# The middle stage of a gated two-layer model on one core: when the row means, the norms' roots and the small inputs are worked on

## The reference

```python
x = x + tanh(g_xattn[0]) * L0_xattn(ctx, ctx, layernorm(x), ssm_kernel, D, 8)   # long convolution per head
x = x + tanh(g_ffn[0])   * L0_ffn(layernorm(x), sim_matrix, gates, w_q, w_k, w_v, o_weights)
x = x + tanh(g_xattn[1]) * L1_xattn(layernorm(x), ctx, ctx)                     # attention, 8 heads
x = x + tanh(g_ffn[1])   * L1_ffn(layernorm(x), w_router, w_fc, w_proj)         # 8 experts, top 2

def L0_ffn(h, sim, gates, w_v, o_weights):          # 32 experts of width 64
    rep = mean(h, axis=1)                           # one row of 512 for each of the 16 sequences
    affinity = (rep / norm(rep)) @ (sim / norm(sim, axis=0))
    gated = relu(affinity - sigmoid(gates)); mask = gated > 0   # with a fallback to the top 16
    routing = softmax(where(mask, gated, -max))     # (16, 32)
    combined = einsum('be,bteh->bth', routing, einsum('btc,ehc->bteh', h, w_v) * mask)
    w_o_dyn  = einsum('be,ehd->bhd', routing, o_weights)
    return einsum('bth,bhd->btd', combined, w_o_dyn)
```

## Time and profile before

| | us |
|---|---|
| median of 3 runs | 1640.89 |
| lowest, highest | 1640.22, 1643.83 |
| profiled execution | 1636.78 |
| its span | 1635.1 |
| granted clock, mean of the span | 0.978 |
| PE busy | 1529.5 (94%) |
| VectorE, ScalarE, POOL busy | 1193.2, 978.7, 1032.5 |

### The profile page before, as it was taken

How to read it: one execution, slowest core, us unless ns; L and a number is a source line. 1 busy time by engine, 2 the same in 40 slices (tenths; PEclk the granted TensorE clock), 3 DMA queues, 4 the chain that set the end, 5 groups by cost and what they waited for, 6 DMA issues and landing times.

```text
span 1635.1 us, 28566 instructions
## 1 busy us (share of the span) xinstructions
PE 1529.5 (94%) x8923; PEld 1073.6 (66%) x8923; DVE 1193.2 (73%) x1863; ACT 978.7 (60%) x1527; POOL 1032.5 (63%) x855
## 2 busy tenths in 40 slices
PE   4999999997698899999999999889999999999996
PEld 4677777775464644444444444368999999999995
DVE  7788888888637667777777777266777777777774
ACT  6433333334624278888888887646777777776773
POOL 4788888885305478888888887601555555555553
PEclk9999999998899999999999999989999999999998
DMA  7333444436634876777777773391444444444443
GB/s 254 113 136 133 134 135 138 141 131 159 178 76 177 194 169 181 185 202 188 184 204 186 189 194 92 115 341 61 70 79 79 77 79 75 76 79 77 78 79 52
DMA packets 110843, 224.27 MB, mean 137 GB/s; under 512 B 12704, under 2 KB 12704, under 8 KB 109856
## 3 DMA queue, kind: packets, MB, share of 16 engines
q1 hardware_dynamic: 94848, 185.88, 40.0%
q0 software_dynamic: 15904, 37.23, 12.8%
HBM read 146.71 MB, written 75.84 MB: 136 GB/s over the span
## 4 chain that ended last, share of the span: by engine, by line
PE 34%; DMA 23%; issue 4%; DVE 3%; ACT 2%; POOL 1%; ACTq 0%; POOLq 0%; SPq 0%; DVEq 0%
DMA out_rows<-XN,slots 21%; PE pB L1433 10%; PE pO L1443 8%; PE pA L1415 7%; PE pO L1456 4%; DMA XN<-normed_rows,slots 1%; PE pO L1606 1%; PE pA L1594 1%; PE pB L1424 1%; POOL out_rows L1399 1%; PE pA L1511 1%; DVE low L1787 1%; PE pO L112 1%; PE pA L1518 0%; DVE XN L1976 0%
## 5 line engine op out<-in xcount | busy, mean ns | idle before, releaser
L1787 DVE TENSOR_REDUCE low<-pA 128x2 f32<-128x1024 f32 x256 | 306.9, 1223 | 112.2 <-PE pA L1415 98.4
L1680 ACT ACTIVATE pt<-pB 128x512 f32<-128x512 f32 x512 | 287.3, 593 | 88.6 <-PE pB L1433 80.4
L436 PE MATMUL y<-kv,toep 128*128 128x288 f32 x1280 | 326.1, 411 | 9.0 <-DVEq L63 5.8
L1399 POOL DMA_INDIRECT out_rows<-XN,slots x71 | 195.6, 2755 | 211.4 <-DMA out_rows<-XN,slots 172.5
L436 PEld LDWEIGHTS y<-kv,toep 128*128 128x128 f32 x1280 | 238.0, 190 | 96.9 <-DVEq L63 34.1
L1594 PEld LDWEIGHTS pA<-XN,fc 128*128 128x128 f32 x2272 | 264.3, 192 | 8.0 <-issue 2.7
L1594 PE MATMUL pA<-XN,fc 128*128 128x128 f32 x2272 | 265.1, 275 | 2.1 <-DVE XN L1956 1.1
L1433 PE MATMUL pB<-qs,ks 98*128 98x512 f32 x512 | 226.9, 446 | 3.7 <-ACT pt L1680 2.4
L1433 PEld LDWEIGHTS pB<-qs,ks 98*128 98x128 f32 x512 | 95.3, 188 | 193.9 <-ACT pt L1680 153.0
L406 ACT ACTIVATE ym<-y 128x384 f32<-128x384 f32 (+1 forms) x128 | 52.5, 410 | 229.0 <-PE y L436 229.0
L1746 ACT ACTIVATE proj_high<-WP 128x2048 fp32r x71 | 135.7, 1912 | 81.4 <-PE pO L1606 81.4
(11 more groups left out here) (285 smaller groups left out, 2509.8 us busy)
## 6 DMA issues: line engine op xcount, KB each, us to landing
ks<-ctx_high SPq DMA_DIRECT2D x64, 256.0 KB, 4.5
qs<-q_high SPq DMA_DIRECT2D x64, 256.0 KB, 6.1
kc<-in_ctx_conv SPq DMA_DIRECT2D x32, 384.0 KB, 5.5
XN<-in_x SPq DMA_DIRECT2D x16, 512.0 KB, 10.4
toep<-kernel_and_skip SPq DMA_DIRECT2D x32, 256.0 KB, 3.5
ct<-in_ctx SPq DMA_DIRECT2D x16, 512.0 KB, 6.3
ctx_high<-kh SPq DMA_DIRECT2D x16, 512.0 KB, 4.4
ctx_low<-kl SPq DMA_DIRECT2D x16, 512.0 KB, 5.1
```

What stands on the lines that cost most here:

```text
L436: m = pe.matmul(y[half].rearrange("p (l n) c -> p l n c", l=CB)[:, l, :, 0:PAIRS], toep[u][:, (l - s) * P:(l - s + 1) * P], kv[u][:, half, ...
L1399: pool.indirect_dma_start(out=out["out"], out_offset=bass.IndirectOffsetOnAxis(ap=slots[:, j:j + 1], axis=0), in_=ys[j % 2], in_offset=Non ...
L1680: act.activation(pt[s][:, h, :], bank(u, n), ACT.Exp, scale=SCALE1).then_inc(s_exp, 1)
L1787: dve.tensor_reduce(ap(low[u % 2], t % CB * NH + t // CB, [[NH, 2], [1, 1]]), pA[n % 2], op=ALU.max, axis=AX.X, negate=True).then_inc(s_re ...
```

## The change

- At the end of the convolution stage PE makes 23 products of the identity with 112 columns of itself into unused columns of y[0], behind s_tt = 2*H0 + 3.
- The groups of roots are now six: (8, 20) is split into (8, 16) and (16, 20). POOL finishes a group behind take(hi + 6) instead of take(hi + 4), the group of rows 24 to 27 behind the loop.
- The last group's roots are finished by VectorE (`last_roots`, with one operation less) right behind its loop; ScalarE makes their guess ahead of keep(31), and its last six weights instead of its last four follow the loop.
- The means' products are issued by fours (`means(i)`): behind forth(15), (17), (23), (25), (27) and (31), the last two fours behind the loop; each waits for its group's spread alone (six of the seven counts).
- The squares of sim and the sigmoid (`early`) stand behind iteration 4 of VectorE's loop, the products for the norms of sim behind forth(7).
- SP waits for five fours instead of two groups before it loads w_o: the same rows, 0 to 19.

```diff
--- before.py
+++ after.py
@@ -440,6 +440,11 @@
                                 if l in (1, 2):
                                     m.then_inc(s_yp, 1)
                             m.then_inc(s_y, 1)
+                unused = 64 - PAIRS
+                pe.wait_ge(s_tt, 2 * H0 + 3)
+                for _ in range(23):
+                    pe.matmul(ap(y[0], PAIRS, [[64, 4], [1, unused]]), ident,
+                              ident[:, 0:4 * unused].rearrange("p (n c) -> p n c", c=unused), start=True, stop=True)
 
             @block.vector
             def _(dve):
@@ -499,8 +504,9 @@
         with ExitStack() as st:
 
             GR = HR // 4
-            GROUPS3 = [(0, 8), (8, 20), (20, 24), (24, 28), (28, 32)]
+            GROUPS3 = [(0, 8), (8, 16), (16, 20), (20, 24), (24, 28), (28, 32)]
             LAST = len(GROUPS3) - 1
+            QUAD_AT = {15: 0, 17: 1, 23: 2, 25: 3, 27: 4, 31: 5}
             PAIRSB = B // 2
             HELD = range(TH, TH + B // 2)
             ORDER = [0] + list(range(1 + PAIRSB // 2, PAIRSB)) + list(range(1, 1 + PAIRSB // 2))
@@ -599,7 +605,7 @@
                     sp.wait_ge(s_x1, TH * b + TH)
                     sp.dma_start(X1[n].rearrange("(th p) c -> p th c", p=P), rows_of(b)).then_inc(s_hold, 16)
                 sp.wait_ge(s_hold, 16 * len(HELD))
-                sp.wait_ge(s_srm, 2)
+                sp.wait_ge(s_srm, (TH * HELD[-1] + TH) // 4)
                 for hq in range(HQ):
                     sp.dma_start(WOin[hq * E0:(hq + 1) * E0], a["w_o"][:, hq * HR:(hq + 1) * HR, :]).then_inc(s_wo, 16)
                 for n in range(HR // GR):
@@ -684,7 +690,7 @@
                 for j in range(3, UNITS):
                     take(j)
                     for g, (lo, hi) in enumerate(GROUPS3):
-                        if j == hi + 4:
+                        if j == hi + 6:
                             first(g)
                     if j == 5:
                         pool.wait_ge(s_ot, j + 1)
@@ -692,7 +698,6 @@
                                            pattern=[[1, E0], [-1, E0]], channel_multiplier=0).then_inc(s_con, 1)
                         pool.wait_ge(s_con, CONS)
                 first(LAST - 1)
-                first(LAST)
                 def add_row(n):
                     j = ROUND[2 * n + 1]
                     pool.wait_ge(s_part, n + 1)
@@ -724,13 +729,21 @@
                         m = pe.transpose(ph[j % 3][:, k * P:(k + 1) * P], ap(XN, j * ROW + k * P, [[1, P]]), ident)
                     m.then_inc(s_t2, 1)
 
-                def means(q):
-                    pe.wait_ge(s_rs, STEPS * (q + 1))
-                    for i in range(GROUPS3[q][0] // 4, GROUPS3[q][1] // 4):
-                        for g in range(4):
-                            m = pe.matmul(pS[g * E0:(g + 1) * E0, :], spread[:, 4 * i + g, :], row(4 * i + g),
-                                          start=(i == 0), stop=(i == UNITS // 4 - 1))
+                def means(i):
+
+                    q = [lo <= 4 * i < hi for lo, hi in GROUPS3].index(True)
+                    pe.wait_ge(s_rs, STEPS * q + STEPS - 1)
+                    for g in range(4):
+                        m = pe.matmul(pS[g * E0:(g + 1) * E0, :], spread[:, 4 * i + g, :], row(4 * i + g),
+                                      start=(i == 0), stop=(i == UNITS // 4 - 1))
                     m.then_inc(s_srm, 1)
+
+                def affinity_norms():
+                    pe.wait_ge(s_e0, 1)
+                    pe.wait_ge(s_con, 5)
+                    for k in range(CB):
+                        m = pe.matmul(p_e, ones, sim2[:, k, :], start=(k == 0), stop=(k == CB - 1))
+                    m.then_inc(s_pe, 1)
 
                 def inner(s):
                     p = ORDER[s]
@@ -756,20 +769,16 @@
 
                 back(0)
                 back(1)
-                pe.wait_ge(s_e0, 1)
-                pe.wait_ge(s_con, 5)
-                for k in range(CB):
-                    m = pe.matmul(p_e, ones, sim2[:, k, :], start=(k == 0), stop=(k == CB - 1))
-                m.then_inc(s_pe, 1)
                 for j in range(UNITS):
                     if j + 2 < UNITS:
                         back(j + 2)
                     forth(j)
-                    for g, (lo, hi) in enumerate(GROUPS3):
-                        if j == hi + 4:
-                            means(g)
-                means(LAST - 1)
-                means(LAST)
+                    if j == 7:
+                        affinity_norms()
+                    if j in QUAD_AT:
+                        means(QUAD_AT[j])
+                for i in range(len(QUAD_AT), UNITS // 4):
+                    means(i)
                 pe.wait_ge(s_ctr, 3)
                 for k in range(CB):
                     m = pe.matmul(p_srt[:, k * B:(k + 1) * B], mid[:, k * P:(k + 1) * P], member, start=True, stop=True)
@@ -821,6 +830,24 @@
                     chain.link(dve.tensor_scalar(t["sig"], t["esig"], 1.0, None, ALU.add))
                     chain.link(dve.reciprocal(t["sig"], t["sig"]))
 
+                def last_roots():
+
+                    lo, hi = GROUPS3[LAST]
+                    steps = Chain(s_rs, dve)
+                    steps.n = STEPS * LAST
+                    r, w, to = guess[:, lo:hi], work[:, lo:hi], rstd[:, lo:hi]
+                    dve.wait_ge(s_rs, STEPS * LAST)
+                    dve.wait_ge(s_gs, 2 * LAST + 2)
+                    steps.link(dve.scalar_tensor_tensor(w, mv[0][:, lo:hi, 1], EPS, r, ALU.add, ALU.mult))
+                    steps.link(dve.tensor_tensor(w, w, r, ALU.mult))
+                    steps.link(dve.tensor_scalar(w, w, -0.5, 1.5, ALU.mult, ALU.add))
+                    dve.sem_inc(s_rs, 1)
+                    steps.n += 1
+                    steps.link(dve.tensor_tensor(to, r, w, ALU.mult))
+                    steps.inc(dve.tensor_copy(ap(spread, lo * E0 + lo // 4, [[4 * E0 + 1, (hi - lo) // 4], [E0, 4]]),
+                                              ap(rstd, lo, [[4, (hi - lo) // 4], [1, 4]])))
+                    steps.link(dve.tensor_scalar(gr[:, lo:hi], to, gates[:, 2:3], None, ALU.mult))
+
                 def sums(n):
 
                     def add(n):
@@ -843,12 +870,14 @@
                     if 0 <= n - 2 < UNITS:
                         close(n - 2)
 
-                early()
                 for n in range(UNITS + 2):
                     sums(n)
+                    if n == 4:
+                        early()
+                last_roots()
                 dve.wait_ge(s_pe, 1)
                 chain.link(dve.tensor_copy(nn[:, 0:E0], p_e))
-                dve.wait_ge(s_srm, LAST + 1)
+                dve.wait_ge(s_srm, UNITS // 4)
                 dve.tensor_reduce(ssum, pS, op=ALU.add, axis=AX.X).then_inc(s_ctr, 1)
                 dve.wait_ge(s_ctr, 1)
                 dve.tensor_scalar(ssum, ssum, 1.0 / C, None, ALU.mult).then_inc(s_ctr, 1)
@@ -959,14 +988,15 @@
                 act.wait_ge(s_in4, 32)
                 act.activation(t["esig"], eg, ACT.Exp, scale=-1.0).then_inc(s_act, 1)
                 for j in range(UNITS):
+                    if j == UNITS - 1:
+                        roots(LAST, 0, *GROUPS3[LAST])
                     keep(j)
                     for g, (lo, hi) in enumerate(GROUPS3):
                         if j == hi + 1:
                             roots(g, 0, lo, hi)
-                    if j >= 4:
+                    if 4 <= j < UNITS - 2:
                         weights(j - 4)
-                roots(LAST, 0, *GROUPS3[LAST])
-                for n in range(UNITS - 4, UNITS):
+                for n in range(UNITS - 6, UNITS):
                     weights(n)
                 act.wait_ge(s_sr, 2)
                 act.activation(ln, nn, ACT.Ln).then_inc(s_act, 1)
```

## The result

The changed kernel takes 1624.99 us (median of 4 runs, 1620.96 to 1629.35) against 1641.54 (4 runs) in the same comparison: ratio 0.9892, 95% interval 0.9864 to 0.9920, or 13 to 22 us less. Against the 1640.89 us of the prediction the ratio gives 1623.2, just under the range's low end of 1624. In a second comparison (6 runs against 17) the ratio was 0.9905 (0.9875 to 0.9936), 15.6 us less. The forecast gain of 13.4 us lies inside both intervals. The profiled execution shown here is a long one: span 1627.3, time 1629.35.

The account below looks back on a forecast made before the run. VectorE was taken to pace the rows loop, with stalls behind PE's turned rows and POOL's wait for ScalarE's guesses. Terms 10.0 - 0.5 + 3.6 + 0.3 = 13.4 us took 1640.89 to 1627.5 us, range 1624 to 1632.

Parts of the forecast that it names:

- Loop: Rows loop up to the reduction over pS: 10.3 us of VectorE stalls fall to 0.3, a gain of 10.0 us.
- Start: First rows: small inputs behind row four stand in the paced loop, a loss of 0.15 to 0.9 us, 0.5 taken.
- Products: End of the convolution stage: 23 products take 3.8 us, end before VectorE's last operation, cost nothing and gain nothing themselves.
- rival B: Attention stage's stirring products end some 5 us early, w_o's products begin at the low clock: 2 us lost, 1629.5; chance 0.09.
- Tail: Last aggregation to the reduction over pS: 3.0 us instead of 6.6, a gain of 3.6 us, bounds 2.7 and 3.9.
- Behind the tail: Products with member and the next ones run faster if PE is still at the high level: 0.3 us gained together.
- w_o: Load of w_o: lands at 445.7 to 446, its reader moves to some 452, six microseconds of cover remain.
- The rule on transposes: Rows loop: by the Trainium skill, transposes leave PE's clock low; the prediction went against it, expecting the high level.
- Rival D: Rows loop: PE runs at the low level, 9 us slower, 1650; chance 0.03.
- C: End of the convolution stage: the 23 products run cold or late and hold the barrier 2.5 us, 1630; chance 0.05.
- A: Rows loop still stalls, 0.7 us at each of four groups: gain 10.6 us, time 1630.3; chance 0.12.
- The total: Whole kernel: 13.4 us gained, 1627.5 us; low end 1624 from favourable ends, 1625.6, with 1.5 us of scatter downward.

Follow-up runs that it names:

- roots_6_alone: Kernel before the change with only POOL's roots moved behind take(hi + 6) and the means to row hi + 7; 1626.87 us in one run.
- early_first: Changed kernel with the small inputs and the products for the norms of sim ahead of the loops again; 1625.44 us, ratio 0.9906.

## Why the prediction was right, and where it was wrong

*Loop: right.* 10.0 us were worked out, 10.2 measured, and by the step named: roots_6_alone gives 9.4 with the later roots and the means that wait for them. POOL's takes were 0.27 us late for PE where 0.1 was reckoned, under the same cover. The expected 0.3 us of stall from the crowded fours did not come.

*Start: right in sign, a little small.* A loss of 0.5 was taken with an end at 0.9; the two profiles show 0.8 and 0.5 at row 5 against the first profile of the kernel before, and early_first gives 0.7 to 1.0. The reason was the one given: take 3 moves with nothing.

*Products: the term was mis-sized.* Nothing was the price, since they would end at 383.1 by twelve passes a microsecond. They ended 0.46 us behind VectorE and cost 0.12 us at the barrier. The step that failed is the reading of the count in the earlier trace rows: a window counts each instruction that touches it, and passes that last 0.275 us and start some 0.11 apart (0.113 here) give eleven or twelve in a window where nine start. 45 steps of 0.113 and the last pass are 5.4 us, not 3.8; the clock was as predicted. The same slip stands in rival B, whose 68 stirring passes, 0.112 us apart at the high level, would take 7.6 us and not 5.7.

*Tail: right in size, wrong in its split.* 3.6 gained as worked out, 3.02 us against the 3.0 of the sum. But not 2 us of it are ScalarE's order: it is 1.3. VectorE in POOL's place is 0.56, PE's wait for one count less 0.3, and 1.4 come from PE's clock and ScalarE's lateness; of these, 0.9 come with the later roots even with the old tail.

*Behind the tail.* 0.3 was taken for the products with member and the next. One profile of the changed kernel has 0.55 (1.34 us instead of the 1.89 of the earlier trace rows), the other nothing (1.89): in the first PE's clock fell to the low level while these products ran (0.50 from 438.9 us on), in the second it was there before they began (0.50 from 436.1 us on).

*w_o: right that it stays hidden, with the cover mis-sized.* Six microseconds were left by the working, 1.4 were (2.2 in the second profile). It was issued at 42.8 us behind the first take instead of the 41.8 that the prediction's times give; above all, the last piece had landed at 451.64 before the change, 22.3 us behind the first issue, and not near 448.5: the window of the earlier trace rows is the last in which packets start, and they take 2.5 us, with the landing 0.6 to 0.7 behind the last one's end. That the reader did not wait owes something to luck.

*The rule on transposes.* The loop of the changed kernel, mostly transposes, ran at 0.99 (1.00 in the second profile). The rule of the Trainium skill, "TensorE: Matmul & The Clock Gate", Part 4: PE-mode transpose, does not hold in this kernel: by the 1.00 of the earlier trace rows with transposes alone, and by this loop. Rival D did not happen. Nor did B, C and A: the stirring took 10.11 us at a low start as before (10.08), C's lateness was 0.12 instead of 2.5, and VectorE waited for nothing.

*The total: the range's low end failed.* The front fell by 13.5 (13.3 in the second profile), the sum said 13.4; that the sum fits so well is in part luck, since its terms for the start and behind the tail missed by about 0.3 each in opposite directions. The measured difference was 17.7 in one comparison and 15.6 in the other, and the first puts the time at 1623.2, 0.8 us below the range. The step of the prediction that failed is the last one, "with the scatter of the runs shown, 1.5 us downward": the term for the scatter was taken from three runs that lay within 3.6 us of one another. The runs show 9 to 12 us in its place: the kernel before from 1636.56 to 1648.65 over 17 runs, the changed one from 1620.56 to 1629.97 over 6, and the kernel before has medians of 1641.54, 1638.88 and, in a third comparison of 11 runs, 1644.13. The prediction also put the later stages at nothing; the profiles have 3.3 us there, with a standard error of 1.4. What part of the 2 to 4 us beyond the front is scatter and what part a real gain in later stages, the runs leave open.

## What to carry to other kernels

When one engine hands out work in its own order, ask for each wait in that order who stands behind it: a slow engine's result asked for two steps too early stopped three others, and moving the question by two rows (and the means that hang on it) was worth 10.2 of the front's 13.5 us. A gain in one part's timing can also bring the clock and the queues of the next part into better shape (0.9 us of the tail here came with the later roots), so undo the parts one by one before dividing the gain. A window that counts instructions or packets counts them where they touch it or where they start: take a rate from the spacing of starts, and a landing from the landing. Before adding work to "start warm", look at what holds the first step: here it was a take on another engine, and PE's warm start bought nothing while that take was late.

## What the runs showed of the hardware

One program's time scatters by up to 12 us in 1640 on one core within a comparison, in part through the granted clock of one stage (110.6 us at 0.92 and 114.4 at 0.90 in two copies of one kernel). The clock held 1.00 over 8 us with nothing but fp32 transposes on PE. Behind a stop of 2.91 us on PE four transposes took 1.11 us instead of 0.60 to 0.66 and a four 1.94 instead of 1.06; with four stops of 9.6 us together in that loop, VectorE waited 11.2 us (clock 0.84 over the loop, 0.99 without stops). Packets of 32 KB take 2.5 us each here, and the last piece of w_o landed 21.6 us behind its issue. And the small dependent operations of a Newton step mostly start 0.26 to 0.31 us apart on GpSimd and 0.20 apart on VectorE; with five of them instead of six up to spread, the last group's roots are 0.56 us sooner there.
